# A per-condition mixing plus low-rank-adapted projection kernel: narrower condition weights, one load for the first input pair, and a separate order for step 1

## What is computed

```python
W = weights[condition]
y = jnp.einsum('bct,bcd->bdt', x, W)
gate_logits = jnp.einsum('bsd,ed->bse', y, gate_w)
weights, selected = jax.lax.top_k(gate_logits, 2)
weights = jax.nn.softmax(weights, axis=2)
result = jnp.einsum('bsd,od->bso', y, base_w) + base_b
w_full = jnp.sum(jax.nn.one_hot(selected, 8) * weights[..., None], axis=2)
low = jnp.einsum('bsd,erd->ebsr', y, lora_A)
lora_out = jnp.einsum('ebsr,eor,bse->bso', low, lora_B, w_full)
return x + result + 2.0 * lora_out
```

## Time and profile before

| what | value |
|---|---|
| median of 3 runs | 499.18 us (499.05 to 501.41) |
| the profiled execution, its own time | 499.68 us |
| its span, first to last instruction | 497.6 us |
| PE busy | 490.4 us (99%) |
| weight loads of PE busy | 481.7 us (97%) |
| ACT busy | 380.6 us (76%) |
| DVE busy | 362.7 us (73%) |
| POOL busy | 123.5 us (25%) |
| granted TensorE clock, mean | 1.000 |
| moved by DMA | 40.07 MB, mean 81 GB/s |

### The profile page before, as it was taken

How to read it: one execution, slowest core, us unless ns; L and a number is a source line. 1 busy time by engine, 2 the same in 40 slices (tenths; PEclk the granted TensorE clock), 3 DMA queues, 4 the chain that set the end, 5 groups by cost and what they waited for, 6 DMA issues and landing times.

```text
span 497.6 us, 8605 instructions
## 1 busy us (share of the span) xinstructions
PE 490.4 (99%) x2792; PEld 481.7 (97%) x2792; DVE 362.7 (73%) x771; ACT 380.6 (76%) x740; POOL 123.5 (25%) x111
## 2 busy tenths in 40 slices
PE   7999999999999999999999999999999999999997
PEld 6989999999999999999999999999999999999997
DVE  4978777778787777777787777787877777777653
ACT  4888878887778787788787788877787877887620
POOL 2033213333113332023331133331133320233120
PEclk9999999999999999999999999999999999999999
DMA  8912121121121221221221211211212212211112
...
DMA packets 11249, 40.07 MB, mean 81 GB/s; under 512 B 1250, under 2 KB 1634, under 8 KB 11234
## 3 DMA queue, kind: packets, MB, share of 16 engines
...
q10 hardware_dynamic: 144, 0.52, 0.3%
...
## 4 chain that ended last, share of the span: by engine, by line
PE 92%; DMA 3%; SPq 1%; DVE 1%; ACT 1%; issue 0%
PE acc L593 77%; PE acc L625 9%; PE mixed L613 5%; DMA x_sb<-in_x 3%; SPq L209 1%; PE acc L619 1%; DVE w_raw L434 0%; ACT w_raw L331 0%; ACT x_parts L326 0%; DVE x_parts L426 0%; ACT y_moved L339 0%; DVE lb_lo L554 0%; SPq L203 0%; DVE w_raw L513 0%; SPq L213 0%
## 5 line engine op out<-in xcount | busy, mean ns | idle before, releaser
L339 ACT COPY y_moved<-w_raw 32x256 f32<-32x256 f32 x480 | 194.0, 404 | 39.3 <-DVE w_raw L434 33.3
L593 PE MATMUL acc<-w_hi,y_hi 128*128 128x384 f32 (+1 forms) x768 | 182.1, 342 | 1.6 <-ACT w_hi L312 1.6
L593 PE MATMUL acc<-w_hi,y_lo 128*128 128x384 f32 (+1 forms) x768 | 179.1, 338 | 0.0
L593 PE MATMUL acc<-w_lo,y_hi 128*128 128x384 f32 (+1 forms) x768 | 179.0, 338 | 0.0
L271 POOL TENSOR_TENSOR w_raw<-x_sb,bias 128x1024 f32<-128x1024 f32 x32 | 77.2, 2413 | 356.0 <-DVE low L490 287.6
L593 PEld LDWEIGHTS acc<-w_hi,y_hi 128*128 128x128 f32 x768 | 135.3, 188 | 9.1 <-issue 2.1
L593 PEld LDWEIGHTS acc<-w_hi,y_lo 128*128 128x128 f32 x768 | 138.6, 188 | 0.0
L593 PEld LDWEIGHTS acc<-w_lo,y_hi 128*128 128x128 f32 x768 | 138.5, 188 | 0.0
L434 DVE TENSOR_TENSOR w_raw<-mixed,w_raw 64x1024 f32<-64x1024 f32 x60 | 73.0, 1217 | 41.6 <-ACT w_raw L331 41.2
L442 DVE STREAM_TRANSPOSE y_turned<-y_moved 128x512 f32<-128x512 f32 x60 | 39.2, 691 | 53.7 <-ACT y_moved L339 53.7
L426 DVE TENSOR_TENSOR x_parts<-x_sb,x_parts 64x1024 fp32r<-64x1024 f32 x60 | 74.0, 1233 | 1.8
...
## 6 DMA issues: line engine op xcount, KB each, us to landing
...
```

The source lines that it names most:

```text
L339: done = nc.scalar.copy(y_moved[q * SQ:(q + 1) * SQ, g, :, :], piece.rearrange("m (k q a) -> m q k a", q=QUARTERS, a=SQ)[:, q, :, :])
L593: return nc.tensor.matmul(acc[:, c % 2, b, 0:hi - lo], y_part[:, c % 2, k, :], w_part[:, k, lo:hi], start=(k == 0 and product == 0), stop= ...
```

## The change

The condition weights come from the host once, on 64 partitions, and are split there. POOL copies both parts of each column half to partitions 64 to 127 (new, two copies of 64 x 2 x 512). Pair 0 of x comes in one load of 512 KB. The first `w_high` goes between the two `y_high_first` of pair 0 on ACT, and the cast of block 0's other columns goes ahead of both `y_low_first` of pair 0 on DVE. Step 1 gets lists of its own on ACT and DVE, with the gating of pair 0 in front, and `x_high` of pair 3 within it; PE issues the two `mix` calls of step 1 after blocks 1 and 3 rather than after blocks 0 and 2. The rest of the program is as before.

```diff
--- before.py
+++ after.py
@@ -49,7 +49,7 @@
     HALF_K = KT // 2
     SQ = 32
     QUARTERS = P // SQ
-    assert cond_w.shape[0] == P
+    assert cond_w.shape[0] == CH
     assert 2 * CH == P and ER == P and T == 2 * 512 and PAIRS % 4 == 0 and O == T
 
 
@@ -79,7 +79,7 @@
         lb_hi = sb("lb_hi", [P, O], F32R)
         lb_lo = sb("lb_lo", [P, O], F32R)
         bias = sb("bias", [P, O], F32)
-        cw = sb("cw", [P, cond_w.shape[1]], F32)
+        cw = sb("cw", [CH, cond_w.shape[1]], F32)
         cw_parts = sb("cw_parts", [P, 2, cond_w.shape[1]], F32R)
         cond_sb = sb("cond_sb", [1, B], I32)
         ident = sb("ident", [P, P], F32)
@@ -126,7 +126,6 @@
         w_in = [sem(f"w_in{k}") for k in range(KT)]
         lb_in = sem("lb_in")
         bias_in = sem("bias_in")
-        x_first = sem("x_first")
         x_in = [sem(f"x_in{i}") for i in range(4)]
         stored = [sem(f"stored{i}") for i in range(4)]
 
@@ -141,6 +140,7 @@
         first_upper = sem("first_upper")
         cw_hi_ready = sem("cw_hi_ready")
         cw_ready = sem("cw_ready")
+        cw_copied = sem("cw_copied")
         ident_zero = sem("ident_zero")
         consts_ready = sem("consts_ready")
 
@@ -202,9 +202,7 @@
             def load_x(j, c):
                 sp.dma_start(x_sb[:, c % 4, :], x_pairs[4 * j + c]).then_inc(x_in[c % 4], 16)
 
-
-            sp.dma_start(x_sb[:, 0, 0:T // 2], x_pairs[0, :, 0:T // 2]).then_inc(x_first, 16)
-            sp.dma_start(x_sb[:, 0, T // 2:T], x_pairs[0, :, T // 2:T]).then_inc(x_in[0], 16)
+            load_x(0, 0)
             for k in range(KT):
                 sp.dma_start(w_raw[:, k, :], w_blocks[k]).then_inc(w_in[k], 16)
                 if k == 0:
@@ -278,10 +276,14 @@
             pool.wait_ge(cw_in, 16)
             pool.wait_ge(w_zero, 1)
             for c in range(2):
-                nc.gpsimd.tensor_copy(w_pair[0:CH, c, 0:CH], cw[0:CH, bass.ds(lower[c] * CH, CH)]) \
+                nc.gpsimd.tensor_copy(w_pair[0:CH, c, 0:CH], cw[:, bass.ds(lower[c] * CH, CH)]) \
                     .then_inc(first_lower, 1)
             pool.wait_ge(first_lower, 2)
-            pool.wait_ge(cw_ready, 2)
+
+            for i, cols in enumerate(CW_HALVES):
+                pool.wait_ge(cw_ready, i + 1)
+                nc.gpsimd.tensor_copy(cw_parts[CH:P, :, cols], cw_parts[0:CH, :, cols]).then_inc(cw_copied, 1)
+            pool.wait_ge(cw_copied, 2)
             select(0, 2)
             pool.wait_ge(bias_in, 16)
 
@@ -359,10 +361,10 @@
 
             act.wait_ge(cw_in, 16)
             for cols in CW_HALVES:
-                nc.scalar.copy(cw_parts[:, 0, cols], cw[:, cols]).then_inc(cw_hi_ready, 1)
+                nc.scalar.copy(cw_parts[0:CH, 0, cols], cw[:, cols]).then_inc(cw_hi_ready, 1)
             y_high_first(0, 0)
+            w_high(0)
             y_high_first(0, 1)
-            w_high(0)
             w_high(1)
             w_high(2)
             w_high(3)
@@ -374,17 +376,28 @@
             x_high(0, 2, first=True)
             act.wait_ge(lb_in, 16)
             nc.scalar.copy(lb_hi[:, :], lb_raw[:, :]).then_inc(lb_hi_ready, 1)
+
+            act.wait_ge(w_ready, 2)
+
+
+            gate_exp(0, 0)
+            rest(0, 2, 0)
             x_high(0, 3, first=True)
-
-            act.wait_ge(w_ready, KT)
+            lowT_high(0, 0)
+            move(0, 2, 0, range(2))
+            rest(0, 2, 1)
+            move(0, 2, 0, range(2, 8))
+            move(0, 2, 1, range(8)).then_inc(moved, 1)
+            y_high(0, 2, 0)
+            y_high(0, 2, 1)
+            x_high(0, 4)
 
             def step(j, c, ahead=True, split=True):
                 if ahead:
                     rest(j, c + 1, 0)
                 gate_exp(j, c - 1)
                 if ahead:
-                    if c >= 2:
-                        act.wait_ge(turned, 8 * j + 2 * (c - 2) + 2)
+                    act.wait_ge(turned, 8 * j + 2 * (c - 2) + 2)
                     move(j, c + 1, 0, range(3))
                     rest(j, c + 1, 1)
                     move(j, c + 1, 0, range(3, 8))
@@ -396,7 +409,7 @@
                 if split:
                     x_high(j, c + 3)
 
-            for n in (1, 2, 3):
+            for n in (2, 3):
                 step(0, n)
             with act.Fori(0, LOOPS) as j:
                 for u in (4, 5, 6, 7):
@@ -519,16 +532,16 @@
             dve.wait_ge(cw_in, 16)
             dve.wait_ge(w_zero, 1)
             for c in range(2):
-                nc.vector.tensor_copy(w_pair[CH:P, c, CH:P], cw[CH:P, bass.ds(upper[c] * CH, CH)]) \
+                nc.vector.tensor_copy(w_pair[CH:P, c, CH:P], cw[:, bass.ds(upper[c] * CH, CH)]) \
                     .then_inc(first_upper, 1)
             for i, cols in enumerate(CW_HALVES):
                 dve.wait_ge(cw_hi_ready, i + 1)
-                nc.vector.tensor_tensor(cw_parts[:, 1, cols], cw[:, cols], cw_parts[:, 0, cols].bitcast(F32),
+                nc.vector.tensor_tensor(cw_parts[0:CH, 1, cols], cw[:, cols], cw_parts[0:CH, 0, cols].bitcast(F32),
                                         ALU.subtract).then_inc(cw_ready, 1)
 
-            y_low_first(0, 0)
             dve.wait_ge(w_in[0], 16)
             nc.vector.tensor_copy(w_hi[:, 0, BW:N], w_raw[:, 0, BW:N]).then_inc(w_first, 1)
+            y_low_first(0, 0)
             y_low_first(0, 1)
             dve.wait_ge(w_first, 1)
             for k in range(4):
@@ -542,6 +555,22 @@
             x_low(0, 2, 1)
             dve.wait_ge(consts_ready, NE)
 
+
+            rank_gates(0, 0)
+            apply_gates(0, 0)
+            add_rest(0, 2, 0)
+            dve.wait_ge(lb_hi_ready, 1)
+            nc.vector.tensor_tensor(lb_lo[:, :], lb_raw[:, :], lb_hi[:, :].bitcast(F32), ALU.subtract) \
+                .then_inc(lb_ready, 1)
+            lowT_low(0, 0)
+            add_rest(0, 2, 1)
+            x_low(0, 3, 0)
+            x_low(0, 3, 1)
+            turn(0, 2)
+            y_low(0, 2, 0)
+            finish(0, 0)
+            y_low(0, 2, 1)
+
             def step(j, c, ahead=True, split=True):
                 rank_gates(j, c - 1)
                 if ahead:
@@ -549,10 +578,6 @@
                 apply_gates(j, c - 1)
                 if ahead:
                     add_rest(j, c + 1, 1)
-                if c == 1:
-                    dve.wait_ge(lb_hi_ready, 1)
-                    nc.vector.tensor_tensor(lb_lo[:, :], lb_raw[:, :], lb_hi[:, :].bitcast(F32), ALU.subtract) \
-                        .then_inc(lb_ready, 1)
                 if split:
                     x_low(j, c + 2, 0)
                 lowT_low(j, c - 1)
@@ -673,9 +698,9 @@
                         for b in range(3):
                             done = project(c, k, b, product)
 
-                    if k == 0 and c == 1:
+                    if k == 1 and c == 1:
                         mix(j, c + 1, 0)
-                    if k == (2 if c == 1 else 1) and ahead:
+                    if k == (3 if c == 1 else 1) and ahead:
                         mix(j, c + 1, 1)
                     if k == 3:
                         transpose_low(j, c - 1)
@@ -716,11 +741,10 @@
             pe.wait_ge(zeros_ready, 1)
             for _ in range(WARM):
                 nc.tensor.matmul(acc[:, 1, 0, 0:P], zeros[:, :], zeros[:, :], start=True, stop=True)
-            pe.wait_ge(x_first, 16)
+            pe.wait_ge(x_in[0], 16)
             pe.wait_ge(first_lower, 1)
             pe.wait_ge(first_upper, 1)
             mix_first(0, 0)
-            pe.wait_ge(x_in[0], 16)
             mix_first(0, 1)
             pe.wait_ge(consts_ready, NE)
             first_step()
@@ -748,7 +772,7 @@
     arrays = {
         "x": x,
         "condition": np.ascontiguousarray(inputs["itok_B_0_15"]).reshape(1, -1),
-        "cond_w": np.ascontiguousarray(np.concatenate([cond_cols, cond_cols])),
+        "cond_w": np.ascontiguousarray(cond_cols),
         "proj_w": np.ascontiguousarray(np.concatenate(
             [base_w, lora_a.reshape(E * R, T), np.asarray(inputs["L0_ffn_gate_w"])]).T),
         "lora_b": np.ascontiguousarray(np.asarray(inputs["L0_ffn_lora_B"]).transpose(0, 2, 1)).reshape(E * R, -1),
```

## The result

The changed kernel takes 502.79 us in the median of 10 runs (501.94 to 503.73), the kernel before 499.97 us in 10 runs beside it (498.77 to 501.73). The ratio is 1.0052 with a 95% interval of 1.0032 to 1.0072: slower by half a per cent, 2.8 us. The forecast of 500.7 us had the direction, but 502.79 lies above its range of 499.2 to 502.4. The profiled execution took 503.21 us, its span is 501.3 us against 497.6, and its mean granted clock 0.996 against 1.000.

A forecast was written before the change was run, and what follows sets the result against it. PE bounds the kernel from 60 to 460 us, so only step 2's start could move: step 1 0.6 us earlier, ACT's last copy 1.5 later, PE at 42.3 against 40.8, +1.5 on 499.18, 500.7 us; range 499.2 to 502.4.

The forecast's parts named there:

- the sum's term for the clock behind the new pause: PE, 39.3 to 42.3 us, ahead of step 2: the sum of +1.5 us added nothing for a slower clock.
- part 1's -0.6 us: Loads and first products: 256 KB fewer ahead of weight block 0, so step 1 starts at about 23.3 instead of 23.89.
- PE and ACT arrive at step 2 together; neither has slack: Start of step 2: a saving on PE alone is worth nothing, a delay of ACT's last copy is paid in full.
- the sum of part 3: ACT in step 1: last copy ends at 38.8 against 37.28; 3.50 us later PE starts step 2, 42.3 against 40.81.
- PE's arrival: PE in step 1: it would reach `mix` of pair 3 at about 23.3 + 15.4 = 38.7, against 40.35.
- The waits of 0.65 and 0.17: PE in step 1: both waits go, as the gating of pair 0 now runs ahead of `add_rest`.
- the rival that came: Clock falls in PE's new pause ahead of step 2: 1.65 us more, 502.4 us; chance 0.13.
- So those casts have left a place where ACT had the time for them: ACT, step 1: pair 3's x casts (2.12 us) now follow `rest`, where ACT has no time; it idles before 27.1.
- the first `rest` waits for a `mix` one block later: ACT in step 1: `rest` starts at 27.1, after a `mix` that stands one block (1.57 us) later.
- block 0 did land earlier: Rival at the start: block 0 does not land earlier, all of step 1 lies 0.6 later, 501.3 us; chance 0.15.
- POOL's copies: Two `cw_parts` copies, 0.6 to 4.8 us, hidden; rival: held up by DVE, above 19.5 us, 502.3 us; chance 0.03.
- PE's start of step 2 was bound by ACT's chain: Rival denied this: PE starts step 2 when it arrives, at 39.2, -1.6, 497.6 us; chance 0.07.

The follow-up runs named there:

- e2_step1_only: The kernel before with only the new order of step 1, loads as before: 504.05 us in 7 runs, ratio 1.0088.
- e3_fill_pause: The changed kernel with 12 matmuls of zeros on PE in the pause ahead of step 2: 501.93 us.
- e5_after_warm12: The changed kernel with 12 instead of 8 matmuls of zeros at the start of PE: 501.78 us.
- e10_loads_warm12: The kernel before with only the loads' part of the change and 12 instead of 8 matmuls of zeros at the start: 498.82 us, ratio 0.9981.
- e11_warm12_fill: The changed kernel with 12 matmuls of zeros at the start and 12 more in the pause ahead of step 2: 500.83 us, ratio 1.0024.
- e4_xcast_first: The changed kernel with the two casts of pair 3's x moved back to the front on ACT: 502.38 us, ratio 1.0047.
- e8_lowT_mix: The changed kernel with the `lowT_hi` cast behind ACT's first eight copies and the `mix` calls back behind blocks 0 and 2: 499.75 us, ratio 0.9994.

## Why the prediction was wrong

**The step that failed is the sum's term for the clock behind the new pause, which was put at nothing, and beside it part 1's -0.6 us.** The first measured 1.64 us in the profile, the second +0.16 us. Either miss alone would have stayed below the upper bound of 502.4 (500.7 + 1.65 = 502.35; 500.7 + 0.75 = 501.45); together they did not. A third share of the distance is no step of the reasoning: the kernel before took 499.97 us in the ten runs beside the changed one, 0.8 more than the 499.18 from which the forecast counts. Against 499.97 the change costs 2.8 us where 1.5 was said.

- **"PE and ACT arrive at step 2 together; neither has slack"** and the sum of part 3 held. From the start of step 1 the prediction had the last copy at 38.8 - 23.3 = 15.5 and PE's start at 19.0; measured 15.5 and 18.97, and again 18.97, 18.97 and 18.98 in three experiments (`e2_step1_only`, `e3_fill_pause`, `e5_after_warm12`). PE's arrival was said to be 15.4 after the start, where the prediction's own 16.46 - 0.82 gives 15.64; it was 15.10, and nothing hung on it. The waits of 0.65 and 0.17 went, the pause was 3.24 us where "some 3" was said.
- **Part 1, "-0.6 us": failed.** S was 24.05, not 23.3. Block 0's missing bytes did bring it earlier (DVE cast it at 7.26 where 7.73 was forecast), but the first mixing began at 5.85, not 5.4, since all of x must land (5.85 to 6.70 in the profiles with one load, 5.40 and 5.59 with two), and then ran at half speed, 3.78 us, until 9.63, for "ends at 7.45". I took its duration from one execution, as if it were fixed. Of the nine profiles with 8 filler matmuls it was 2.05 us in four and 3.18 to 3.79 in five; the kernel before's own spread of 499.05 to 501.41 us, which stood ahead of the prediction, was a sign of such draws. The term is off by 0.75 us in the profile. With the mixing at full speed it would have been off the other way: in `e10_loads_warm12` and `e11_warm12_fill`, where x landed at 5.86 and 5.88, S was 22.80 and 22.81, 0.5 earlier than forecast.
- **The clock was the rival that came, and its chance was the error.** It was priced at 1.65 us and cost 1.64 in the profile, but it was given 0.13. That the price fits is partly luck: it was read from 16 passes at the start, and in `e2_step1_only` the same pause cost 2.8. All ten runs of the changed kernel have a clock of 0.993 to 0.997. `e11_warm12_fill`, where it stays up, takes 500.83 us, beside the forecast of 500.7; that nearness is luck too, since its S is 0.5 us earlier than forecast and the kernel before was slower than the 499.18 of the sum. The argument against, that a pause of 1.58 us had left no trace, told nothing of one of 3.24. "TensorE: Matmul & The Clock Gate" of the Trainium skill (Part 1) stood against the forecast, and the runs agree with it in kind, with the addition that behind one and the same pause of 3.24 us the clock does not fall every time.
- **"So those casts have left a place where ACT had the time for them": wrong as a reason**, although the sum was right. `e4_xcast_first` shows that they hide behind the wait for the transpose. The step had counted both, 2.12 us for the casts and 0.5 for the wait, and they cover each other: less of one is more of the other. The other half of the reasoning, that the first `rest` waits for a `mix` one block later, held: with that and the cast of `lowT_hi` undone (`e8_lowT_mix`) the last copy came 2.2 us earlier.
- The other rivals: block 0 did land earlier; POOL's copies took 2.67 us for both, inside the 0.6 to 4.8 of the bounds, and held nobody up; PE's start of step 2 was bound by ACT's chain, as said.

Together: 2.2 us by the start of step 2 (0.16 from S, 2.05 from step 1) and 1.64 by the clock are 3.85; the two spans differ by 3.7.
